# A recurrent block and two FFNs on one core: the second FFN starts in round 14 with two units a round, W1 and W2 are split later, the front is reordered

## The reference

```python
t  = rmsnorm(x) * norm1_w
xb = causal_depthwise_conv(t @ Wx, conv_w, conv_b)          # 4 taps over tokens
a  = exp(-8 * softplus(lam) * sigmoid(xb @ Wa))
b  = sqrt(max(1 - a * a, 1e-12)) * sigmoid(xb @ Wi) * xb
h  = scan over the tokens: h = a * h + b
h1 = x + (h * gelu(t @ Wy)) @ Wo
u  = rmsnorm(h1) * norm2_w
x1 = layernorm(x + h1 + (gelu(u @ Wg) * (u @ Wu)) @ Wd)     # first FFN, hidden size 1024
y  = layernorm(x1 + relu(x1 @ W1 + b1) @ W2 + b2)           # second FFN, hidden size 1024
```

## Time and profile before

| | before |
|---|---|
| median of 3 runs | 600.15 us (599.4 to 600.36) |
| the profiled execution | 600.54 us |
| its span, first to last instruction | 598.7 us |
| PE busy | 590.6 us, 99% of the span, 3529 matmuls |
| DVE busy | 381.5 us, 64% |
| ACT busy | 317.2 us, 53% |
| POOL busy | 187.1 us, 31% |
| granted PE clock | 0.999 of full speed over the span |

### The profile page before, as it was taken

One profiled execution on the slowest core, in us unless ns is written; L12 is line 12 of the kernel. 1 busy time (PEld: TensorE's weight loads), 2 busy tenths in 40 slices (PEclk: granted clock), 3 DMA queues, 4 the chain that ended last, 5 costly groups with the idle time before them and its releaser, 6 DMA issues.

```text
span 598.7 us, 9284 instructions
## 1 busy us (share of the span) xinstructions
PE 590.6 (99%) x3529; PEld 521.7 (87%) x3529; DVE 381.5 (64%) x700; ACT 317.2 (53%) x601; POOL 187.1 (31%) x287
## 2 busy tenths in 40 slices
PE   8999999999999999999999999999999999999996
PEld 7768888899888998889898988889888898889896
DVE  5889877374856567484774846857478474662565
ACT  5988853654438444375443744356444653323454
POOL 3041353117240352313513153140722215240130
PEclk9999999999999999999999999999999999999999
DMA  8530010001001010010100001010000100010011
GB/s 283 166 106 1 1 36 1 2 1 36 1 1 35 2 37 0 1 36 2 35 2 19 18 1 36 1 36 2 1 1 0 37 2 0 2 36 0 1 37 36
DMA packets 13100, 15.68 MB, mean 26 GB/s; under 512 B 616, under 2 KB 12288, under 8 KB 13056
## 3 DMA queue, kind: packets, MB, share of 16 engines
q1 hardware_dynamic: 13056, 15.09, 7.5%
HBM read 10.89 MB, written 4.19 MB: 25 GB/s over the span
## 4 chain that ended last, share of the span: by engine, by line
PE 91%; DVE 5%; ACT 1%; issue 1%; DMA 1%; POOL 1%; SPq 0%; DVEq 0%
PE psum L361 17%; PE psum L363 17%; PE psum L362 17%; PE psum L372 11%; PE psum L374 11%; PE psum L373 11%; PE psum L379 3%; DMA xs<-in_L_attn_x_dram 1%; PE psum L447 1%; PE psum L575 1%; PE psum L577 1%; PE psum L573 1%; DVE row L1285 1%; PE psum L474 1%; PE psum L414 1%
## 5 line engine op out<-in xcount | busy, mean ns | idle before, releaser
L1662 POOL TENSOR_SCALAR gu_hi<-gu_raw 128x512 fp32r<-128x512 f32 x64 | 52.8, 824 | 313.1 <-DVE gu_raw L1308 310.3
L1318 DVE TENSOR_TENSOR hid_lo<-hid_raw,hid_hi 128x512 fp32r<-128x512 f32 x56 | 45.6, 814 | 84.0 <-ACT hid_hi L952 84.0
L948 ACT ACTIVATE hid_raw<-psum,vecs 128x512 f32<-128x512 f32 x56 | 38.5, 687 | 113.8 <-PE psum L363 113.8
L1308 DVE TENSOR_TENSOR gu_raw<-psum,gu_raw 128x512 f32<-128x512 f32 x64 | 44.1, 689 | 68.4 <-PE psum L363 68.1
L372 PE MATMUL psum<-w_d_hi,gu_hi 128*128 128x256 f32 x256 | 72.8, 284 | 0.2 <-DVE gu_lo L1313 0.2
L372 PE MATMUL psum<-w_hi,hid_hi 128*128 128x256 f32 x256 | 71.7, 280 | 0.2 <-DVE hid_lo L1318 0.2
L374 PE MATMUL psum<-w_hi,hid_lo 128*128 128x256 f32 x256 | 71.8, 281 | 0.0
L374 PE MATMUL psum<-w_d_hi,gu_lo 128*128 128x256 f32 x256 | 71.8, 281 | 0.0
L373 PE MATMUL psum<-w_lo,hid_hi 128*128 128x256 f32 x256 | 71.7, 280 | 0.0
L373 PE MATMUL psum<-w_d_lo,gu_hi 128*128 128x256 f32 x256 | 71.7, 280 | 0.0
L939 ACT ACTIVATE gu_raw<-psum 128x512 f32<-128x512 f32 x64 | 38.3, 598 | 48.6 <-PE psum L363 48.0
(11 more groups left out here) (222 smaller groups left out, 1519.3 us busy)
## 6 DMA issues: line engine op xcount, KB each, us to landing
out_dram<-row SPq DMA_DIRECT2D x15, 256.0 KB, 2.2
xs<-in_L_attn_x_dram SPq DMA_DIRECT2D x7, 512.0 KB, 3.5
raw<-in_L_ffn_W_dram SPq DMA_DIRECT2D x2, 1024.0 KB, 7.9
raw_gud<-in_L_attn_Wg_dram SPq DMA_DIRECT2D x1, 1024.0 KB, 7.4
raw_gud<-in_L_attn_Wu_dram SPq DMA_DIRECT2D x1, 1024.0 KB, 9.5
raw_gud<-in_L_attn_Wd_dram SPq DMA_DIRECT2D x1, 1024.0 KB, 12.7
xs<-in_L_attn_x_dram SPq DMA_DIRECT2D x2, 256.0 KB, 2.9
raw_xyai<-in_L_attn_Wx_dram SPq DMA_DIRECT2D x1, 256.0 KB, 2.6
```

The source lines that it names most:

```text
L948: nc.scalar.activation(hid_raw[:, w % SLOTS, :], bank[:, :], ACT.Relu, bias=vec("b1", m)).then_inc(relu_ready, 1)
L1308: nc.vector.tensor_tensor(gu_raw[:, r % SLOTS, :], up_bank(r)[:, :], gu_raw[:, r % SLOTS, :], ALU.mult).then_inc(gu_ready, 1)
L1318: nc.vector.tensor_tensor(hid_lo[:, w % SLOTS, :], hid_raw[:, w % SLOTS, :], hid_hi[:, w % SLOTS, :].bitcast(FP32), ALU.subtract).then_inc ...
L1662: nc.gpsimd.tensor_scalar(gu_hi[:, r % SLOTS, :], gu_raw[:, r % SLOTS, :], 1.0, 0.0, ALU.mult, ALU.add).then_inc(gu_hi_ready, 1)
```

## The change

In words, part by part:

1. **Front.** The mean square of x is finished on ACT (Sqrt) and DVE (reciprocal) instead of POOL. DVE takes the first half of the scaled transposes and ACT the second (they swap). The half gates alternate Wa and Wi. Wx of chunk 1 is issued by its k half, around Wo. The splits of Wg and Wu move behind the recurrence; DVE norms three of the four tiles of u and ACT one.
2. **Rounds 0 to 7.** `gate(1)` comes ahead of `up(0)`, `down` trails by two units instead of one and stands between `gate(r)` and `up(r)`, and Wa and Wi of chunk 1 move from round 3 to round 4. The sum of x and h1 of chunk 0 moves from POOL to DVE (`first_add_x`, round 3).
3. **W1 and W2.** The raw halves of W1 and all of W2 are loaded into freed space of Wg, Wu and Wd and a half-size buffer; they are split in rounds 9 to 13. The load of W2 waits for Wd's split.
4. **Second FFN.** It begins in round 14 with units 0 and 1, then two units a round up to round 17, and one a round from 18 on (w = r-10, as before). Wo of chunk 2 moves from round 13 to round 14, between `mlp_up(1)` and `mlp_down(0)`, and u of chunk 2 is transposed in round 15 behind `mlp_down(1)`.
5. **Banks.** Gate and up use banks 4 and 5 in rounds 9, 11 and 13 as well; from round 18 on gate uses bank r mod 2, up the other one, and `mlp_up(w)` bank w mod 2, so that it waits for gelu (`gelu_ready`) and not for the multiply.

The core of the diff:

```diff
+        PACED = KH + LAG_UP
+        ASIDE = (1, 3, 5, 9, 11, 13)
+        def second_units(r):
+            if r < FROM:
+                return ()
+            if r < PACED:
+                return (2 * (r - FROM), 2 * (r - FROM) + 1)
+            return (r - LAG_UP,)
         def gate_bank(r):
-            return psum[SECOND] if r in (1, 3, 5) else psum[GATE]
+            if r < PACED:
+                return psum[SECOND] if r in ASIDE else psum[GATE]
+            return psum[r % 2]
...
             def first_period(r):
-                gate_up(r)
-                if r in (1, 5):
-                    pe.wait_ge(hi_split["d"], 1 + r // 5)
-                    pe.wait_ge(lo_split["d"], 1 + r // 5)
-                if 1 <= r < KH - 1:
-                    down(r - 1)
-                if r == 3:
+                if r != 1:
+                    gate(r)
+                if r == 0:
+                    gate(1)
+                if r in (2, 6):
+                    pe.wait_ge(hi_split["d"], 1 + r // 6)
+                    pe.wait_ge(lo_split["d"], 1 + r // 6)
+                if r >= 2:
+                    down(r - 2)
+                if r == 4:
                     split_done("a", "i")
                     mix_decay(1)
                     mix_input(1)
+                up(r)
...
-                if r == LAG_UP:
-                    split_done("1")
...
-                if units(r - LAG_UP):
-                    mlp_up(r - LAG_UP)
-                if units(r - LAG_DOWN):
-                    mlp_down(r - LAG_DOWN)
+                if r == FROM:
+                    split_done("1", "2")
+                for w in second_units(r):
+                    mlp_up(w)
+                    if w == 1:
+                        mix_out(n)
+                    if w >= 1:
+                        mlp_down(w - 1)
+                    if w == 2:
+                        transpose_u(n)
...
+            def first_add_x():
+                dve.wait_ge(first_u_ready, TT - 1)
+                dve.wait_ge(u_ready, u_tiles(0))
+                for q in range(PAIRS):
+                    total = pair_of(h1[0], q)
+                    nc.vector.tensor_tensor(total, total, pair_of(xs[0], q), ALU.add).then_inc(first_xh_ready, 1)
...
-                if units(r - LAG_UP):
-                    hidden_lo(r - LAG_UP)
-                if r == LAG_UP:
+                for w in second_units(r):
+                    hidden_lo(w)
+                    if w == 2:
+                        split_lo(uT_lo, uT_hi, uT_hi_ready, uT_lo_ready, n)
+                if r == KH + 2:
+                    weight_lo("1", ks=[0])
+                if r == KH + 3:
+                    weight_lo("1", ks=[1])
+                if r == KH + 4:
+                    weight_lo("2", ks=[0])
+                if r == KH + 5:
                     weight_lo("2", ks=[1])
```

More of the change, by code:

```diff
@@ L77, in griffin_mlp_kernel @@
         h1.append(sb("h1_1", [P, TT, D]))
-        with nc.sbuf_tensor("raw_2", [P, WIDTH], FP32) as raw:
-            raw_of["2"] = raw[:, :]
-        rows = [sb(f"row{i}", [P, TT, D]) for i in range(2)]
+        rows = [sb("row0", [P, TT, D])]
+        with nc.sbuf_tensor("raw_1", [P, H], FP32) as raw:
+            raw_1 = [raw[:, :]]
+        rows.append(sb("row1", [P, TT, D]))
         normed = sb("normed", [P, TT, D])
@@ L695, in round_of @@
                     mix_decay(n)
-                if mixing and m == 7 and p >= 1:
+                if mixing and m == 7 and p >= 2:
                     transpose_u(n)
@@ L719, in round_of @@
                     mix_y(n)
-                if mixing and m == 5 and p >= 1:
+                if mixing and m == 5 and p >= 2:
                     mix_out(n)
@@ L742, in _ @@
                 first_y(h)
-            second_x(0)
+            for m in range(KD):
+                second_x(m, 0)
             pe.wait_ge(w_loaded["o"], DMA)
@@ L770, in square_first_x @@
                     last.then_inc(x_squared, 1)
+                    tiles = slice(2 * q, 2 * q + 2)
+                    act.wait_ge(rms_eps_ready, 1)
+                    act.wait_ge(x_squared, q + 1)
+                    nc.scalar.activation(rstd1[:, tiles], ss1[:, tiles], ACT.Sqrt, bias=rms_eps[:, :],
+                                         scale=1.0 / D).then_inc(rms1_ms, 1)
             def square_x(c):
@@ L1069, in _ @@
             nc.scalar.activation(vecs[:, :], psum[UP][:, 0:NV], ACT.Copy).then_inc(vecs_ready, 1)
+            act.preload_act_table(ACT.Exp)
             act.wait_ge(vecs_ready, 1)
@@ L1433, in round_of @@
                     scan_both(n)
-                if m == 6 and mixing:
+                if m == (7 if p == 1 else 6) and mixing:
                     for q in range(PAIRS):
@@ L1489, in lam_stepped @@
                 dve.wait_ge(lam_step, steps)
-            first_norm_t(0)
+            for q in range(PAIRS):
+                first_norm_t(q)
+            dve.wait_ge(vecs_ready, 1)
+            dve.wait_ge(tT_done, 1)
+            for f in range(KD):
+                nc.vector.tensor_scalar(first_tT[0][:, f, half(0)], pair_bank(MIX, 0)[:, f, :], vec("n1", f), None,
+                                        ALU.mult).then_inc(first_tT_ready[0], 1)
             dve.wait_ge(lam_exp, 1)
@@ L1499, in _ @@
             lam_stepped(nc.vector.scalar_tensor_tensor(poly, poly, series[3], z, ALU.add, ALU.mult))
-            dve.wait_ge(vecs_ready, 1)
-            dve.wait_ge(tT_done, 2)
-            for f in range(KD):
-                nc.vector.tensor_scalar(first_tT[0][:, f, half(1)], pair_bank(MIX, 1)[:, f, :], vec("n1", f), None,
-                                        ALU.mult).then_inc(first_tT_ready[1], 1)
             for c in (2, 1):
```

254 lines of the change are left out of this document (158 added, 96 removed).

## The result

The changed kernel takes 602.36 us (median of 6, 602.27 to 602.5), the one before 599.72 us (median of 6, 599.4 to 600.36). The ratio is 1.0044, with a 95% interval of 1.0032 to 1.0055: slower by 0.4%. The profiled execution took 602.32 us with a span of 600.53 us. That is 1.8 us more than the profiled one of before, while the medians are 2.6 us apart, because the profiled execution of before was 0.8 us longer than its median (more on that under the experiments).

A forecast was written before the change was run, and what follows sets the result against it. PE, busy 99%, bounds the kernel, so only its waits count: 600.54 - 0.25 (up to round 8) - 1.08 - 0.4 + 3.7 (new waits) = 602.5, forecast 602.2 us against the median; range 599.0 to 603.6.

The forecast's parts named there:

- The front: Ahead of round 0: PE's waits for the convolution and gy go; 1.1 us gained (0.5 to 1.5), round 0 at 34.95.
- `down(0)` and `down(1)`: Rounds 0 on: a wait of 0.4 us with its 0.08 stays, and a second of 0.1 comes at down(1).
- the chain up, multiply, hi, lo took 3.1 us: Round 0: time from the end of up(0) to 42.48; two products of 1.38 now stand in it, leaving 0.4 us.
- Wa to Wo: Chunk 1: 21.5 us, not shorter than 21.61, set by ACT; PE waits 0.8 us at gate(7) and again for Wo's input.
- To round 8: After Wo of chunk 1: the 9.8 us stay within 0.1, taken as 9.7; round 8 begins at 83.45.
- `down(8)`: Round 8: both statistics on DVE delay the multiply of unit 8; PE waits 0.75 and 0.11 against 0.27.
- `down(13)`: Round 13: chain from gate(12) through Sqrt, gy and lo takes 14.65 us, PE has 13.8; 0.9 lost with the resume.
- W2: Round 14: mlp's mT_lo twice and the second half's split stand behind the lo part on DVE; PE waits 0.9 us.
- `hid_lo` of unit 6: Round 17: multiply to end of hid_lo takes 6.2 us on DVE, behind the taps; PE waits 1.0 us.
- more arise: Rival: in round 16 hid_lo of unit 4 is late behind sums and statistics; 0.5 to 1.5 us more, 603.5; chance 0.13.
- 537 us: Behind round 18: the alternating banks take away PE's wait of 0.4 us at 537.18 and no other.
- four waits of 4 us: Upper end of the main case, four waits of 3 to 4 us in rounds 8 to 17: 601.4 to 603.2, chance 0.5.

The follow-up runs named there:

- run 8: The kernel before, unedited, timed and profiled once more: 599.71 us, ratio 0.9997, span 598.0 us; round 0 begins at 35.48.
- run 6: The changed kernel, with ACT squaring x of chunk 2 behind the gelu of unit 6 and not ahead of it: 602.46 us, ratio 1.004.
- run 10: The changed kernel, with one more small product and power of constants on POOL in round 5, ahead of chunk 2's power: 602.96 us, ratio 1.0056.
- run 1: The changed kernel, with PE waiting for W2's second half only ahead of the first mlp_down, not ahead of mlp_up(0): 601.45 us, ratio 1.0022.
- run 2: The changed kernel, with DVE making hid_lo of unit 6 between taps (round 17) and of unit 4 between statistics (round 16): 601.16 us, ratio 1.002.
- run 5: The changed kernel with all five waits of rounds 8 to 17 attacked by reordering, W2's second half split in round 14: 598.51 us, ratio 0.9976.
- run 7: The changed kernel, with W2's second half split twice on DVE, the first result written over: 603.55 us, ratio 1.0064.
- run 9: Banks of before from round 18 on: in the changed kernel 602.87 us, in the kernel with five waits attacked 598.91 us.
- run 3: The changed kernel with four reorderings: later W2 wait, earlier hid_lo, unit 13's lo part ahead of both h products, unit 8's multiply earlier: 601.96 us, ratio 1.0026.
- run 11: The kernel of run 5, with chunk 1's Wo and gy's hi parts ahead of chunk 2's t, squares of x later: 599.5 us, ratio 0.9997.

## Why the prediction was right

I forecast 602.2 us, and 602.36 came. Point by point:

- **The front**, 1.1 us. The two profiles show 1.57 (34.51 against 36.08), but 0.6 of it is the execution of before that I read. Against run 8 it is 0.97, from one trace of each kernel. The steps came as forecast: PE no longer waits for the convolution or for `gy`, and it waits 0.33 us at 32.47 for u. ACT's table load is followed by the next instruction with no gap (1.28 us at 6.20, next at 7.49), so the drain that the Trainium skill (ScalarE: Activation LUTs, What ACT_TABLE_LOAD costs) puts on top is not seen here.
- **`down(0)` and `down(1)`**, 0.4 and 0.1 us. Wrong: neither exists (41.49 follows without a gap, round 0 to Wa takes 16.93 us). The step that failed is "the chain up, multiply, hi, lo took 3.1 us", kept at that size. From the end of `up(0)` to the end of lo it took 2.8 us before (39.40 to 42.22, and 0.26 more to the start of `down(0)`), and it takes 2.5 here (38.76 to 41.23), since POOL's hi takes 0.62 us and not 0.98. With the same 0.26 that fits into the two products. DVE stands idle beside it for 0.82 us, where before it had a tap to do.
- **Wa to Wo**, 21.5 us. It took 21.56, and the 0.8 at `gate(7)` came. But the cause that I gave, that ACT sets it, holds at most for its first half. That ACT's table loads and Sqrt set the scan is read from the order and was not tested. Behind it run 6 shows that the squares and the gelu of unit 6 are not on the chain, since moving them leaves Wo at 73.00, and ACT then waits for POOL's power. My prediction didn't have that power (1.86 us) in this chain, though the kernel before has it too (1.87 us at 68.84). Run 10 agrees, with a shift of only 0.3 us.
- **To round 8**, 9.7 us: 9.61.
- **`down(8)`** 0.86, measured 0.7; **`down(13)`** 0.9, measured 0.85; **W2** 0.9, measured 1.2; **`hid_lo` of unit 6** 1.0, measured 1.1. That these are the causes is shown by taking each away (runs 1, 2, 5) and for W2 by doubling it (run 7). The rival "more arise" came in part: `hid_lo` of unit 4 waited 0.37. Sum 4.2 against 3.7. The two that missed most are the wait of unit 4, which the sum put at nothing, and W2's, whose sum had no resume and no hand-over (DVE's split ends at 121.75, PE starts at 122.12).
- **537 us**, 0.4 us won: shown by run 9. Not seen ahead: the wait at 488, 0.34. It comes and goes with what happens before round 18 (run 5 does not have it); why, stays open.

So the mechanism of rounds 8 to 17 was right, but that the time came out to 0.2 us is luck: two errors cancel. All up to round 8 was 0.8 us better than forecast (82.61 against 83.45; 0.44 of it ahead of round 0, 0.4 behind), and the waits behind were 0.8 worse (4.2 and 0.34 against 3.7). The distance to before is larger than forecast, 2.6 us between the medians against 2.05, because I started from an execution of before whose front was 0.6 us late. With run 8's trace in its place, round 8 begins 0.43 us earlier by the change, and -0.43 - 1.1 - 0.4 + 4.2 + 0.34 is 2.6, against 2.6 between the spans (600.53 and 597.96). One range in the prediction doesn't follow from its own terms: four waits of 4 us give 602.4 us and not 603.2.

In one sentence: the change starts the second FFN later, so that rounds 8 to 13 have 4.2 us of PE work each in which DVE and ACT must bring the next operand, and it puts the left-over DVE work (statistics, W2's split, two `hid_lo` behind statistics and taps) on just these chains.

## What to carry to other kernels

When PE is busy all the time, a change of order is worth what it does to PE's starts alone: list for each moved step which instruction PE needs next, what stands ahead of it in its engine's queue, and how many products PE has until then. A late operand can often be cured by moving one instruction forward in one queue (run 2: two lo parts moved forward, 1.2 us), but look at all that waits for what is pushed back, on every engine, and at what a wait was hiding (run 3: 0.85 us became 2.0). A profiled execution can lie 0.8 us from the median in its front, and 1.85 in run 11; compare distances between two starts behind the front, and profile the kernel before twice when tenths matter.

## What the runs showed of the hardware

A small power on POOL (128x4) has no fixed price. Twelve of the 13 in the changed kernel took 1.01 to 1.05 us, and the one at 67.95 took 1.86; at that place it took 1.85 to 1.87 in the other traces too, but 1.35 and 1.01 in run 10. The product before it took 0.70 in the changed kernel, 0.19 and 0.24 in run 10. DVE is busy beside the slow ones: in the changed kernel with a lo part from 67.12 and a scan from 67.73 to 69.01, and the power of 1.01 us in run 10 starts at 69.29, behind the scan's end at 69.22. Beside the powers at 130.03 and 134.54 (1.02 and 1.01 us) DVE stands still. But beside the one at 12.75 (1.05 us) DVE runs taps, which read psum, so that DVE is busy is not enough. Whether it is the kind of DVE's work that makes the difference, no run tried.

A long stand of PE may cost granted clock as well. In run 3, whose longest stand is 2.1 us at 120 us, eight of 12 executions had a granted clock of 0.995 to 0.997 and took 1.6 us more than the other four. In run 7, with 2.5 us, one of five did so (605.24 us at 0.995). In the kernels whose longest stand behind the front is under 1.3 us the clock was never under 0.998. That the stand is the cause is a guess from these numbers; the traces that I have of these kernels are of executions with the full clock, so it was not seen where the clock fell. Against it stands that the kernel before, which has no such stand, also took 1.2 to 1.6 us more in four of 35 executions (601.09 to 601.46 us), at 0.998, a clock at which others took the usual 599.7. A late front, as in run 11's trace, can cost as much, and no trace rules it out for run 3.

The front waits for transfers that land at varying times: x of chunk 1 in run 8, and in the profile of run 2 PE waited for Wi:

```profile
12.40 1.97 PE L497 MATMUL psum<-xb,raw_xyai 128*128 128x256 f32 x8 [1.24 <-DMA raw_xyai<-in_L_attn_Wi_dram]
```

The alternating half gates need Wi one k half earlier than before the change. So that execution had round 0 at 35.70 and a time of 601.99 us, against a median of 601.16.
